# Last global slots of a macaron kernel: an exponential and three divisions change place on ScalarE and VectorE

## The reference

```python
x = x + 0.5 * ffn(layernorm(x))     # first stack, depth 2
x = x + attn(layernorm(x))          # global attention
x = x + 0.5 * ffn(layernorm(x))     # second stack, the same weights
```

```python
qk = q @ k.T                        # (1024, 1024) for each sequence
theta = 0.5 + 0.2 * sigmoid(qk) + 0.15 * tanh(qk) + 0.1 * relu(qk)
out = softmax(theta) @ v            # then Wo and bo
```

## Time and profile before

| | us |
|---|---|
| median of three runs | 3062.69 |
| the profiled execution, its time | 3062.09 |
| its span, first to last instruction | 3060.3 |
| TensorE matmul busy | 2986.1 (98%) |
| VectorE busy | 2588.4 (85%) |
| ScalarE busy | 2093.9 (68%) |
| GpSimd busy | 1748.7 (57%) |
| mean granted TensorE clock | 0.993 |

### The profile page before, as it was taken

One profiled execution on the slowest core, in us unless ns is written; L12 is line 12 of the kernel. 1 busy time (PEld: TensorE's weight loads), 2 busy tenths in 40 slices (PEclk: granted clock), 3 DMA queues, 4 the chain that ended last, 5 costly groups with the idle time before them and its releaser, 6 DMA issues.

```text
span 3060.3 us, 84552 instructions
## 1 busy us (share of the span) xinstructions
PE 2986.1 (98%) x30773; PEld 2157.1 (70%) x30773; DVE 2588.4 (85%) x5526; ACT 2093.9 (68%) x5016; POOL 1748.7 (57%) x1158
## 2 busy tenths in 40 slices
PE   7999999999999999989999799999999999999999
PEld 4777777667777777656777577777766677777765
DVE  7999998668888888858999699999866788888866
ACT  4777777436777777328889477777753677777742
POOL 8888886125666665541000688888721566666610
PEclk9999999999999999999999899999999999999999
DMA  5222222102222232100000122222320122222221
GB/s 131 50 50 52 51 57 63 45 18 48 51 49 52 50 64 60 41 1 1 1 1 1 24 52 52 51 51 56 65 52 14 43 50 52 50 52 58 57 49 42
DMA packets 311515, 138.26 MB, mean 45 GB/s; under 512 B 225897, under 2 KB 276546, under 8 KB 311106
## 3 DMA queue, kind: packets, MB, share of 16 engines
q1 hardware_dynamic: 311106, 132.84, 19.9%
HBM read 28.13 MB, written 19.66 MB: 16 GB/s over the span
## 4 chain that ended last, share of the span: by engine, by line
PE 90%; DVE 4%; issue 2%; POOL 2%; ACT 1%; SPq 0%; DMA 0%; DVEq 0%; ACTq 0%; POOLq 0%
PE psum L1264 14%; PE psum L1139 11%; PE psum L1238 8%; PE psum L1285 7%; PE psum L1296 7%; PE psum L1316 7%; PE psum L1194 6%; PE psum L1165 5%; PE psum L1226 5%; PE psum L1330 3%; PE psum L1346 3%; PE psum L1529 3%; PE psum L1505 3%; PE psum L1184 3%; PE psum L1515 2%
## 5 line engine op out<-in xcount | busy, mean ns | idle before, releaser
L491 POOL TENSOR_TENSOR rnorm<-ssq_floor,neg_half 128x16 f32<-128x16 f32 x256 | 750.7, 2932 | 491.0 <-DVE qkr L813 486.2
L566 ACT ACTIVATE shared<-psum,neg_max 128x128 f32<-128x128 f32 x2048 | 596.6, 397 | 39.8 <-DVE neg_max L789 39.8
L496 POOL TENSOR_TENSOR qk_cos<-qk_cos,qk_sin 128x1024 f32<-128x1024 f32 x256 | 607.3, 2372 | 0.0
L1264 PE MATMUL psum<-wqkv,hT 128*128 128x512 f32 x1024 | 532.2, 603 | 17.7 <-DVE qk_sin L775 9.5
L587 ACT COPY shared<-psum 128x512 f32<-128x512 f32 x256 | 150.3, 587 | 435.0 <-PE psum L1226 435.0
L775 DVE TENSOR_TENSOR qk_sin<-psum,sin 128x512 f32<-128x512 f32 x512 | 350.5, 685 | 97.9 <-ACT sq L573 96.6
L780 DVE TENSOR_TENSOR qk_cos<-psum,cos 128x512 f32<-128x512 f32 x512 | 350.6, 685 | 78.6 <-ACT sq L573 78.4
L625 ACT ACTIVATE shared<-psum,b1g 128x512 f32<-128x512 f32 (+1 forms) x192 | 131.7, 686 | 355.2 <-PE psum L1139 352.0
L1139 PE MATMUL psum<-shared,w1g 128*128 128x512 f32 (+1 forms) x768 | 347.2, 595 | 5.4 <-DVE shared L879 4.0
L573 ACT ACTIVATE sq<-psum 128x512 f32<-128x512 f32 x512 | 334.6, 654 | 25.2 <-PE psum L1264 25.2
L1296 PEld LDWEIGHTS psum<-wo,shared 128*128 128x128 f32 x2048 | 267.5, 191 | 115.7 <-issue 115.0
(11 more groups left out here) (132 smaller groups left out, 6382.5 us busy)
## 6 DMA issues: line engine op xcount, KB each, us to landing
vprev<-v SPq DMA_DIRECT2D x512, 130.0 KB, 2.3
token_blocks<-blocks SPq DMA_DIRECT2D x236, 64.0 KB, 1.6
hT<-token_blocks SPq DMA_DIRECT2D x944, 16.0 KB, 1.8
shared<-Y SPq DMA_DIRECT2D x32, 256.0 KB
shared<-Y SPq DMA_DIRECT2D x32, 224.0 KB
out<-X SPq DMA_DIRECT2D x8, 512.0 KB, 3.2
X<-in_L_attn_x SPq DMA_DIRECT2D x7, 512.0 KB, 6.5
wqkv<-in_L_ffn_wqkv SPq DMA_DIRECT2D x4, 512.0 KB, 3.9
```

Source lines behind the costliest of these rows:

```text
L491: nc.gpsimd.tensor_tensor(rnorm[:], ssq_floor[:], neg_half[:], ALU.pow).then_inc(rnorm_ready, 1)
L496: nc.gpsimd.tensor_tensor(both, both, qk_sin[:, t.m % 2, :], ALU.add).then_inc(sum_ready, 1)
L566: last = nc.scalar.activation(probs[:, c * P:(c + 1) * P], bank(3 + i, (c % 4) * P, (c % 4 + 1) * P), ACT.Exp, bias=neg_max[:, c:c + 1])
L1264: nc.tensor.matmul(bank(i), hT[:, t.m * P:(t.m + 1) * P], wqkv[:, i * INNER:(i + 1) * INNER], start=True, stop=True).then_inc(qk_psum, 1)
```

## The change

Two blocks of `global_slot` become functions, and each is called from another place in the last slots. On ScalarE, the exponential of query tile 63 stood first in slot 64; now it stands in slot 63, between the copies of tile 62's transposed shares and `local_slot(2, -4)`. On VectorE, the divisions of query tiles 61, 62 and 63 stood first in slots 64, 65 and 66; now they stand in slots 63, 64 and 65, directly ahead of the `local_slot` of that slot. The additions to X (L1061) stay in slots 64 to 66. TensorE, GpSimd and SyncE have the same streams as before, and every wait and every instruction is the same.

```diff
 # ScalarE
+            def shares_of(t):
+                q = t.m % 2
+                if t.k == 0:
+                    act.wait_ge(pv_ready, NT * DEPTH)
+                    act.wait_ge(hid_ready, 3 * NG * DEPTH)
+                wait(act, bias_ready, t.k + 1)
+                wait(act, pT_psum, 2 * (t.k - 1))
+                nc.scalar.activation(g_probs[:, q, :], theta[:, q, :], ACT.Exp, bias=bias_top[:, q:q + 1],
+                                     scale=0.1).then_inc(g_probs_ready, 1)
+
             def global_slot(k):
-                if t := query_at(k - 1):
-                    ... (the same lines)
+                if (t := query_at(k - 1)) and early_tile(k - 1) < -4:
+                    shares_of(t)
...
                 if early_tile(k) >= -4:
+                    if t := query_at(k):
+                        shares_of(t)
                     local_slot(DEPTH, early_tile(k))
 # VectorE
+            def averages(t):
+                q = t.m % 2
+                acc = bank(6, 0, P + 1)
+                wait(dve, out_psum, t.k + 1)
+                nc.vector.reciprocal(g_rsum[:, q:q + 1], acc[:, P:P + 1]).then_inc(g_rsum_ready, 1)
+                wait(dve, g_rsum_ready, t.k + 1)
+                nc.vector.scalar_tensor_tensor(out=g_out[:, q, :], in0=acc[:, 0:P], scalar=g_rsum[:, q:q + 1],
+                                               in1=bo_all[:], op0=ALU.mult, op1=ALU.add).then_inc(g_o, 1)
+
             def global_slot(k):
                 if k <= 0:
                     residual(group_at(DEPTH - 1, NG - 1 + k))
-                if t := query_at(k - 3):
-                    ... (the same lines)
+                if (t := query_at(k - 3)) and early_tile(k) <= -4:
+                    averages(t)
...
                 if early_tile(k) >= -4:
+                    if t := query_at(k - 2):
+                        averages(t)
                     local_slot(DEPTH, early_tile(k))
```

More of the change, by code:

```diff
@@ L699, in prepare @@
                                    ).then_inc(vo_ready, 1)
-            def global_slot(k):
-                if t := query_at(k - 1):
[L703 to L710, removed]
+            def shares_of(t):
[7 more added lines that the diff above has]
+                                     scale=0.1).then_inc(g_probs_ready, 1)
+            def global_slot(k):
+                if (t := query_at(k - 1)) and early_tile(k - 1) < -4:
+                    shares_of(t)
                 if t := query_at(k + 1):
```

## The result

The changed kernel takes 3050.42 us (median of seven runs, 3048.88 to 3052.04) against 3062.69 (3058.3 to 3063.12); the ratio of the two is 0.9964, 95% interval 0.9952 to 0.9975. The forecast was 3050.7. The profiled execution took 3050.42 us with a span of 3048.6, 11.7 less than before.

The account below looks back on a forecast made before the run. TensorE, nine tenths of the chain, bounds the kernel; time is won where it idles or loses clock, in the hand-over to the second stack. 13.2 less 1.2 is 12.0: 3062.09 becomes 3050.1, median 0.6 above, 3050.7; range 3046 to 3058.5.

Parts of the forecast that it names:

- Third division: Division of query tile 63 on VectorE, gone from before the norms of tile 1: worth 0.55 us.
- thin stretch: TensorE at about 1712 to 1715.5, eight transposes of tile 0 and waits, where the clock was taken as likely to fall.
- The term of 1.2: Low clock for projection and values of tile 3 makes the key transposes 1.2 us late, taken off 13.2.
- a guess for the lower end: GpSimd instructions run longer beside a busier VectorE; 1 us a slot in two or three slots leaves 9 to 10.
- 13.2: Gain in us at GpSimd's power of tile 3, from 1742.13 to 1728.9, before the clock's cost.
- Clock low throughout: Rival, 22%: TensorE's clock stays low through the hand-over, 8.1 us won, 3054.6.
- gain absorbed: Rival, 10%: VectorE's or GpSimd's stream catches off the path, power of tile 3 starts near 1742 again, 3060 to 3065.
- slower: Rival, 6%: TensorE loses its clock as the second stack starts, two slots at half clock cost 16 us, 3067.
- The rule on transposes: Skill rule weighed against the change: if it holds, transposes before the product of tile 62 will not keep the clock up, 3054.6.
- the term on GpSimd: GpSimd's line of sum, normalisations, floors and power in the hand-over: free by 1728.5 for the power of tile 3.

Follow-up runs that it names:

- third division back: Changed kernel with the division of query tile 63 back at the head of its old slot, the other moves kept; 3050.81 us.
- epsilon first: Changed kernel with GpSimd's small addition of epsilon (L508) put ahead of the sum of the rotation in slots -4 to -1; 3047.91 us, ratio 0.9956.
- deferral of three units: Changed kernel with the normalisation units of slots -3 to -1 taken out, rows s+8 and s+9 normalised in each even slot from 0; 3088.28 us, ratio 1.0088.
- two units deferred: Changed kernel with the normalisation units of slots -2 and -1 taken out, rows s+10 and s+11 normalised in each even slot from 0; 3044.72 us, ratio 0.9946.

## Why the prediction was right

*Place and order.* Each start up to tile 1's norms came within 0.4 us: exponential 1695.25 (said 1695.4), product 62 at 1699.60 (1699.9), product 63 at 1705.11 (1705.3), norms of tile 0 at 1710.02 (1710.3), of tile 1 at 1716.76 (1717.1), key transposes at 1719.66 (1719.7). 0.15 of each difference is the span's earlier start of the work.

*Exponential and first division as a pair.* I had given both to the product of tile 62 and no price to either. The runs show 0.14 for the exponential alone and 4.7 for exponential and two divisions without the first (98.06 - 93.36): each uncovers the other's wait. Of the first division's 6.85, some 3 are low clock that comes back with the wait (2.44 and 3.78 us instead of 1.95 and 1.96, values 1.73 instead of 1.02), the rest is the wait itself.

*Third division.* Priced at 0.55 by its leaving the place ahead of tile 1's norms. It is 0.44 on the ruler, but not by tile 1's norms, which start with the end of GpSimd's sum either way (1716.76, and 1716.91 with the division back). It comes from tile 0's norms, 0.5 later with the division in front of them, and from what they meet on GpSimd: the floor (0.96) and not the two normalisations (2.73). The right size, by another way than forecast.

*The clock.* It did fall in the thin stretch, and tile 3's projection took 3.59, as said; but it was back for the values (1.02), so the key transposes were not late. The term of 1.2 is 0. The first scores ran at full clock, so the maxima came at 1725.07, 1.2 ahead of the forecast. Two stretches of the kernel after, then of the run with the divisions alone (columns as in the earlier trace rows):

```profile
1694.00:1718.00 24.00, 18.05 (x85) 11.55 (x84) 18.93 (x41) 10.42 (x24) 16.22 (x12) 0.93 0.11 25
1718.00:1742.00 24.00, 19.17 (x189) 12.87 (x191) 18.83 (x38) 14.85 (x40) 22.74 (x20) 0.93 0.21 46
```

```profile
1694.00:1718.00 24.00, 16.74 (x83) 11.06 (x82) 17.36 (x40) 9.99 (x22) 13.95 (x12) 0.97 0.10 23
1718.00:1742.00 24.00, 17.75 (x178) 11.33 (x180) 18.80 (x39) 14.42 (x39) 22.65 (x21) 1.00 0.22 49
```

The second kernel had the better clock (0.97 and 1.00 against 0.93 and 0.93) and the same 9.58 us from power to power: from tile 1's power on, the low clock costs nothing in the hand-over as it is now. GpSimd is busy for 22.7 of 24 us in the second stretch of both. Ahead of tile 1's power it does cost: 1.5 us in the run with epsilon first.

*GpSimd.* That is the other step that was mis-sized. I let it be free at 1728.5, just ahead of the norms of tile 2, and had stretched instructions only as a guess for the lower end. It was free at 1730.5: L508 took 1.31 instead of 0.23 twice, on the way of tiles 1 and 2. The gain was capped at 11.6 and not at 13.2. So 13.2 - 1.2 = 12.0 hit 11.55 by two errors that cancel: a cost of the clock that was none, and one of GpSimd that was left out of the sum. The path up to tile 1's norms was right; that the total came out within half a us was luck.

*The rivals.* Clock low throughout, gain absorbed, slower: none came. The part of the second that would have been right is the place: a stream not on the path took over, but late, and left 11.55 of 13.2.

*The rule on transposes.* The product of tile 62, at full clock, stands directly behind eight transposes, themselves at full clock (1.04 us). So transposes in front did not bring the clock down here, and the first half of what the Trainium skill says ("TensorE: Matmul & The Clock Gate", Part 4: PE-mode transpose), that the full clock does not engage for them, does not agree with this trace; what they count for is not shown.

## What to carry to other kernels

Two waits in front of one instruction are worth nothing one by one: look for the second before you price the first (exponential alone 0.14, with the divisions 1.7). When two kernels are closer than their executions are to each other, measure from a landmark behind which the edits begin: medians gave 2.5 us to an edit that the traces give 0.7. When a chain that goes through all engines is shortened, ask which engine's own work is the next floor, and price it with durations beside the new neighbours, not with those taken from beside an idle engine. When work is moved later to take that floor down, count the lead in slots of the slowest of the engines: with a lead of one slot the deferral of three units cost 38 us, with three slots that of two gained 4.6 on the ruler.

## What the hardware showed that I had not expected

Small GpSimd instructions that start together with or within VectorE's norms (SBUF to SBUF, 128 x 1024, 1.18 to 1.31 us) end with them: L508 at 1716.76 took 1.31 and ended at 1718.07, the norms at 1717.99; the floor L488 at 1710.39 took 0.96 and ended at 1711.35, the norms at 1711.24. Those that had started ahead of the norms did not: the floor in the run with two units deferred, and the power of 0.71 with epsilon first, 0.33 ahead:

```profile
1724.72 0.25 POOL L490 TENSOR_SCALAR ssq_floor<-ssq 128x16 f32<-128x16 f32 x1
```

```profile
1724.84 1.23 DVE L820 TENSOR_TENSOR qkr<-qk_cos,rnorm 128x1024 f32<-128x1024 f32 x1
```

That it is the order of the starts, and not the operation, was not tried by an experiment of its own, but the same instruction shows it elsewhere in that trace. Two floors of the first stack, and the norms beside them:

```profile
35.52 1.17 POOL L490 TENSOR_SCALAR ssq_floor<-ssq 128x16 f32<-128x16 f32 x1
...
44.92 0.76 POOL L490 TENSOR_SCALAR ssq_floor<-ssq 128x16 f32<-128x16 f32 x1
```

```profile
35.38 1.18 DVE L820 TENSOR_TENSOR qkr<-qk_cos,rnorm 128x1024 f32<-128x1024 f32 x1
...
44.24 1.31 DVE L820 TENSOR_TENSOR qkr<-qk_cos,rnorm 128x1024 f32<-128x1024 f32 x1
```

Started 0.14 and 0.68 after the norms, they take 1.17 and 0.76, and both end 0.1 after them. It is not only the small ones: of the normalisations of one row (L516, 0.79 alone), 48 start within norms in the kernel after; they take 1.15 to 1.68, and all end 0.67 to 0.68 after the norms. A start just ahead is no safe cover: a small power that began 0.04 ahead of the norms, at 77.34 in the kernel after, took 1.80 instead of 0.71, and with the third division back the second of the two normalisations at 1708.41 began 0.14 ahead (1709.21 against 1709.35) and took 1.94. And VectorE is held up as well. Its addition to X, 0.27 alone, took 1.32 in the run with two units deferred, beside GpSimd's sum, which ran from 1712.82 to 1715.17:

```profile
1714.00 1.32 DVE L1070 TENSOR_TENSOR X<-X,g_out 128x128 f32<-128x128 f32 x1
```

The Trainium skill ("GPSIMD Engine Reference", 8. Key points) says that GpSimd shares its SBUF interfaces with VectorE and contends with VectorE instructions that have two SBUF inputs; the norms are such an instruction (qk_cos and rnorm), and the traces agree for what starts within them, 1.31 us instead of 0.23, and for the addition to X, whose inputs X and g_out lie in SBUF too. I had not weighed this rule in the prediction, where it belonged to the term on GpSimd.
